# Attention values by one 129-column product for three of four blocks, and normalised outputs written by the vector engine

## The reference, cut to what matters

```python
x = x + s * g                      # first layer: linear attention, experts, routed experts
xn = _layernorm(x)
s = _L1_attn_ref(xn, qkv, q_bias, positional, out_kernel, out_bias)   # the stage changed
g = _silu(_L1_ffn_ref(xn, W_r, W_k, W_v, mu_r, mu_k))
x = x + s * g
```

## Time and profile before

| what | value |
|---|---|
| time, median of 3 runs | 1228.07 us (1223.23 to 1232.13) |
| profiled execution | 1229.18 us, of which the span is 1227.2 us |
| mean granted TensorE clock | 0.985 |
| TensorE products busy | 1162.7 us (95%) |
| VectorE busy | 821.1 us (67%) |
| GpSimd busy | 825.2 us (67%) |
| ScalarE busy | 681.0 us (55%) |

### The profile page before, as it was taken

The page is one execution under the profiler, slowest core; times in us unless marked ns, Lnnn a source line. Parts: engine busy times, 40 slices in busy tenths (PEclk is TensorE's granted clock), DMA queues, the critical chain, the costliest instruction groups (busy, mean ns, idle before and its releaser), DMA issues.

```text
span 1227.2 us, 31272 instructions
## 1 busy us (share of the span) xinstructions
PE 1162.7 (95%) x11854; PEld 762.0 (62%) x11862; DVE 821.1 (67%) x2026; ACT 681.0 (55%) x1374; POOL 825.2 (67%) x1097
## 2 busy tenths in 40 slices
PE   4899899989898999999999999999999999999997
PEld 2355466757574666766666666676666666566665
DVE  3778768613476786687578668668757866866552
ACT  2534343226414566666656666666665666666665
POOL 1778300130516588798797788888879879888895
PEclk9999889989999999999999999999999999999998
DMA  8200200022103402222031140221203104023001
GB/s 319 115 1 1 74 5 1 9 69 77 36 14 77 117 15 45 44 55 45 19 79 24 23 88 10 45 58 41 45 19 79 36 11 88 11 45 68 14 2 36
DMA packets 74753, 60.10 MB, mean 49 GB/s; under 512 B 38950, under 2 KB 69162, under 8 KB 73516
## 3 DMA queue, kind: packets, MB, share of 16 engines
q1 hardware_dynamic: 73580, 56.02, 18.5%
q0 software_dynamic: 1024, 2.09, 0.6%
HBM read 19.70 MB, written 4.72 MB: 20 GB/s over the span
## 4 chain that ended last, share of the span: by engine, by line
PE 66%; ACT 2%; DVE 2%; issue 1%; DVEq 0%
PE S L1875 10%; PE S L1876 10%; PE S L1877 9%; PE A L1865 9%; PE O L1889 5%; PE O L1890 5%; PE O L1887 5%; PE M L1856 2%; PE M L1833 2%; PE M L1835 2%; PE M L1834 2%; PE M L1850 1%; PE M L1843 1%; PE M L1841 1%; PE M L1842 1%
## 5 line engine op out<-in xcount | busy, mean ns | idle before, releaser
L1617 POOL TENSOR_TENSOR plow<-prob 128x512 f16<-128x512 f32 (+3 forms) x640 | 589.1, 932 | 93.6 <-ACT prob L2091 70.0
L2091 ACT ACTIVATE prob<-S,keep_sigma 128x512 f32<-128x512 f32 (+3 forms) x640 | 396.1, 626 | 264.5 <-PE S L1877 261.6
L2192 DVE CUSTOM_DVE_ANT_0 junk<-A,mask_rows,part 128x512 bf16<-128x512 f32 (+3 forms) x384 | 249.0, 648 | 98.1 <-PE A L1865 77.6
L1887 PE MATMUL O<-V,prob 128*128 128x65 f16 x2176 | 232.7, 193 | 0.2 <-POOL plow L1617 0.2
L1889 PE MATMUL O<-V,prob 128*128 128x64 f16 x2176 | 232.5, 194 | 0.0
L1890 PE MATMUL O<-V,plow 128*128 128x65 f16 x2176 | 231.6, 192 | 0.0
L1875 PE MATMUL S<-rows 97*128 97x512 f16 (+3 forms) x640 | 223.1, 349 | 3.8 <-ACT prob L2091 3.5
L1865 PE MATMUL A<-rows 96*128 96x512 f16 (+3 forms) x640 | 221.0, 346 | 1.3 <-DVE part L2192 1.0
L1876 PE MATMUL S<-rows 96*128 96x512 f16 (+3 forms) x640 | 222.3, 347 | 0.0
L1877 PE MATMUL S<-rows 96*128 96x512 f16 (+3 forms) x640 | 220.7, 345 | 0.0
L1887 PEld LDWEIGHTS O<-V,prob 128*128 128x128 bf16 x2176 | 203.0, 97 | 23.6 <-POOL plow L1617 0.3
(11 more groups left out here) (365 smaller groups left out, 1880.8 us busy)
## 6 DMA issues: line engine op xcount, KB each, us to landing
rows<-stage_rows SPq DMA_DIRECT2D x64, 256.0 KB, 3.4
V<-stage_v SPq DMA_DIRECT2D x16, 516.0 KB, 4.7
W<-in_W SPq DMA_DIRECT2D x2, 2048.0 KB
shifted<-turned SPq DMA_DIRECT2D x32, 128.0 KB, 2.3
rows<-stage_pos SPq DMA_DIRECT2D x64, 64.0 KB, 3.1
w<-in_w SPq DMA_DIRECT2D x2, 1024.0 KB
xe_rows<-zero SPq DMA_DIRECT2D x1, 1280.0 KB, 9.1
ye_rows<-xe SPq DMA_DIRECT2D x5, 256.0 KB, 3.2
```

The lines of the kernel that those rows point to most:

```text
L1617: pool.tensor_tensor(plow[:, k % PB, 0:w], full, full.bitcast(BF16).rearrange("p (q e) -> p q e", e=2)[:, :, 1], ALU.subtract).then_inc(s_ ...
L1887: pe.matmul(both, high[:, cs, 1], vh[h][:, j, 0:HS + 1], start=(j == 0 and s == 0), stop=False, skip_group_check=True)
L2091: act.activation(prob[:, k % PB, 0:w], S[k % 2][:, 0:w], ACT.Exp, scale=sigma[:, 2 * p + h:2 * p + h + 1]).then_inc(s_exp, 1)
L2192: dve.tensor_tensor_reduce(junk[:, g % 2, 0:w], A[g % 2][:, 0:w], add, -1.0, before, ALU.add, ALU.min, out).then_inc(s_max, 1)
```

## The change

The `O` bank now holds, for the blocks s = 0, 1, 2 (APART = 3), 129 columns each (64 sums of high values, the sum of weights, 64 sums of low values) and for block 3 the 65 columns as before; 3 x 129 + 65 = 452 of 512 columns. For the three blocks the two products with high weights become one of 129 columns. ScalarE no longer writes outputs: `scaled` is gone. VectorE, in the slot where it inverted the sums (m+8), takes two inversions, scales the low part and the high part of three blocks, scales block 3, and adds the low part.

```diff
+APART = TPC - 1
+        lows = sb("low_outputs", [P, APART, HS])
                 for s in range(r, TPC):
                     cs = slice((s - r) * P, (s - r + 1) * P)
-                    at = s * (HS + 1)
+                    at = s * VW
                     both, part = O[c % 2][:, at:at + HS + 1], O[c % 2][:, at:at + HS]
-                    pe.matmul(both, high[:, cs, 1], vh[h][:, j, 0:HS + 1], start=(j == 0 and s == 0), stop=False,
-                              skip_group_check=True)
-                    pe.matmul(part, high[:, cs, 1], vh[h][:, j, HS + 1:VW], start=False, stop=False, skip_group_check=True)
+                    if s < APART:
+                        pe.matmul(O[c % 2][:, at:at + VW], high[:, cs, 1], vh[h][:, j, :], start=(j == 0 and s == 0), stop=False,
+                                  skip_group_check=True)
+                    else:
+                        pe.matmul(both, high[:, cs, 1], vh[h][:, j, 0:HS + 1], start=False, stop=False, skip_group_check=True)
+                        pe.matmul(part, high[:, cs, 1], vh[h][:, j, HS + 1:VW], start=False, stop=False,
+                                  skip_group_check=True)
                     ins = pe.matmul(both, plow[:, n % PB, cs], vh[h][:, j, 0:HS + 1], start=False, stop=j == TPC * c + s,
                                     skip_group_check=True)
...
-            def scaled(p, m):
...
-                act.wait_ge(s_rec, g + 1)
-                for s in range(TPC):
-                    ins = act.activation(otok[:, TPC * c + s, HS * h:HS * (h + 1)],
-                                         O[c % 2][:, s * (HS + 1):s * (HS + 1) + HS], ACT.Copy,
-                                         scale=rsum[:, c % 2, s:s + 1])
-                ins.then_inc(s_otok, 1)
...
-                if n >= SCALE:
-                    scaled(*divmod(n - SCALE, SLOTS))
...
                     dve.wait_ge(s_pv, SLOTS * p + m + 1)
-                    sums = O[c % 2][:, 0:TPC * (HS + 1)].rearrange("p (s v) -> p s v", v=HS + 1)[:, :, HS]
-                    dve.reciprocal(rsum[:, c % 2, :], sums).then_inc(s_rec, 1)
+                    g = 2 * NC * p + NC * h + c
+                    blocks = O[c % 2][:, 0:APART * VW].rearrange("p (s v) -> p s v", v=VW)
+                    last = O[c % 2][:, APART * VW:APART * VW + HS]
+                    r, to = rsum[:, c % 2, :], otok[:, TPC * c:TPC * (c + 1), HS * h:HS * (h + 1)]
+                    each = r[:, 0:APART].unsqueeze(2).to_broadcast([P, APART, HS])
+                    dve.reciprocal(r[:, 0:APART], blocks[:, :, HS])
+                    dve.reciprocal(r[:, APART:TPC], O[c % 2][:, APART * VW + HS:APART * VW + HS + 1]).then_inc(s_rec, 1)
+                    dve.wait_ge(s_rec, g + 1)
+                    dve.wait_ge(s_otok, g + 1)
+                    if h == 0 and c == 0:
+                        dve.wait_ge(s_item, count(turn_item(plan[p == PAIRS - 1], -1, 3), p)[0])
+                    dve.tensor_tensor(lows[:], blocks[:, :, HS + 1:VW], each, ALU.mult)
+                    dve.tensor_tensor(to[:, 0:APART, :], blocks[:, :, 0:HS], each, ALU.mult)
+                    step(dve.tensor_scalar(to[:, APART, :], last, r[:, APART:TPC], None, ALU.mult))
+                    dve.tensor_tensor(to[:, 0:APART, :], to[:, 0:APART, :], lows[:], ALU.add).then_inc(s_otok, 1)
```

## The result

| kernel | median us | against the kernel before, 95% interval |
|---|---|---|
| before | 1229.33 (6 runs) | |
| changed | 1237.57 (6 runs, 1234.35 to 1239.25) | 1.0068 (1.0049 to 1.0087) |

A forecast was written before the change was run, and what follows sets the result against it. TensorE's back-to-back stream of products was taken as the bound. 1229.18 - 8.4 (merged product) + 2.4 (VectorE's group work) - 0 (ScalarE) - 0.8 (end) = 1222.4, given as 1222 us; range 1215 to 1237 us.

The forecast's parts named there:

- Part 1, the product: TensorE's value products: a merged block takes 87.0 ns, 5.5 less, over 1536 blocks; gain 8.4 us, range 0 to 10.3.
- Rivals 3 and 4: Merged product: 3, it saves nothing, 1231 us, chance 0.14; 4, its weight load is unhidden, 1270 us, chance 0.02.
- Part 2, the price of the group work: VectorE's added work at group ends: 1.32 us net per group, bounds 1.2 and 1.7, 64 groups, 84 us.
- the surcharge of the addition: VectorE's 192-column addition, both inputs in SBUF, beside a working GpSimd: 0.04 us on top of 0.28, at worst 0.16.
- Part 2, the path: TensorE waiting on VectorE's delayed maxima near slots 7 and 19: 0.3 to 0.35 us a pair, 2.4 us in all.
- The capacity of the `A` link: Row-score products wait for the maximum of two tiles before; slots 19 and 7 can take 1.2 us each.
- several slots: Items and joins behind the delayed maxima on VectorE's queue have this long until someone needs them.
- Part 3, ScalarE's stall: Slot 50 of each pair: the 0.6 us stall goes, but VectorE's maximum holds the same time; value 0, at most 4.9 us.
- The end: Last inversion to transpose: 2.28 us before, then 1.41 us and a signal of 0.06; 0.8 us less.
- Rival 1: VectorE becomes the bound at the eight group ends; with 2.0 us net per group 1248 us; chance 0.14.

The follow-up runs named there:

- e1: The changed kernel with only the merging undone (high weights of blocks 0 to 2 take two products again); 1243.73 us, ratio 1.0117.
- e2: The kernel before with the merged product alone; ScalarE writes outputs as before, low part left out for blocks 0 to 2; 1222.33 us, ratio 0.9955.
- e4: The changed kernel with the addition folded into three 64-column VectorE instructions that take the high part from PSUM, same result; 1226.36 us, ratio 0.9982.
- e3: The changed kernel without VectorE's last addition, so the low part is left out of the outputs; 1222.17 us, ratio 0.9952.
- e5: The changed kernel with VectorE only copying the low part and adding the high part from the bank, ScalarE scaling one slot later; 1222.82 us, ratio 0.9944.

## Why the prediction was wrong

**Part 1, the product: right, a fifth too much.** The merged block is 87 ns as forecast. Over a pair the value products give 0.83 us, which is 6.6 us for eight pairs, not 8.4. The difference is in the blocks left alone: between other blocks block 3 takes 95.4 ns from start to start where it took 92.0, and as the last of a stretch its first two distances are 66.3 ns against 61.7. In e1, with the same bank layout but no merged product, it is 92.0 again, so it comes with the merged products; why is open. e1 (6.2, with 6.8 in the value products) and e2 (5.4 against the run of before beside it, 6.5 in the stage) agree with 6 to 7. Rivals 3 and 4 fell: products of 129 columns with a load each stand 57.6 ns from the next. This also disagrees with the 81 ns that the Trainium skill, "TensorE: Matmul & The Clock Gate", section "Back-to-back issue gap", gives for 128 columns in such a stream.

**Part 2, the price of the group work: this is the step that failed.** The term was the surcharge of the addition, "scaled to 192 columns that is 0.04, at worst 0.16". The rows that I scaled had 64 x 512 elements and a median of 805 ns against 692, and I took the difference for a slower rate. It is a wait for GpSimd's instruction to end; it doesn't shrink with the columns. Measured: a mean of 0.23 us, 0.5 at slot 19 and 0.7 at slot 51.

The trace of the kernel before had it already. One of the 28 instructions of the earlier trace rows, and GpSimd beside it:

```profile
659.16 1.03 DVE L2166 TENSOR_TENSOR shifted<-turned,shifted 64x512 f32<-64x512 f32 x1
```

```profile
658.60 1.04 POOL L1617 TENSOR_TENSOR plow<-prob 128x512 f16<-128x512 f32 x1 [0.48 <-ACT prob L2091]
```

GpSimd ends at 659.64 and the join at 660.19. 27 of the 28 last, within 7 ns, the longer of 674 ns and what GpSimd's instruction still needs plus 542 ns. Only the part behind the wait shrinks with the columns, from 542 ns for 512 to 214 for 192; the median of 805 was a mixture of instructions that waited and that did not.

The rest of the sum held: 1.38 us without the surcharge, against 1.37 in mine. Inside it block 3 took 0.31 us for 0.24, since 208 ns was the price with a constant and not with a pointer scalar, and the inversions and scalings were 0.06 cheaper. The Trainium skill, "SBUF — State Buffer", section "Who interferes with whom", says that a VectorE instruction with two SBUF inputs contends with a GpSimd instruction that reads SBUF, and that the order of issue decides who blocks; that the first one holds the shared ports for its whole instruction it says of VectorE's 2-port modes. I cited it for the kind and not for the amount. The trace agrees, and shows the whole instruction for two SBUF inputs too: ends 0.21 to 0.24 us behind GpSimd's in 51 of 56 cases.

**Part 2, the path: right in the link, short by one.** The capacity of the `A` link holds nearly: at slot 19 I had 1.2 us; the net work there was 1.29 + 0.5 = 1.8 and the stall 0.68, which makes it 1.1, and e4 gives the same (1.33 net, 0.23 of stall). But the list had only the `A` buffers. The banks `M`, which VectorE frees with its item instructions, add 0.42 us a pair; I had given these "several slots". With both links slot 19 takes only about 0.8 us from the first inversion to the next maximum: work of 1.88 us (changed kernel), 1.42 (e4) and 0.98 (e3) delays TensorE there by 1.06, 0.61 and 0.16 us. That e5, planned against 1.2 us, stays clear with its 0.78 is in part luck.

**Part 3, ScalarE's stall: right.** It went, and came back as a wait on the maximum at the next slot; in e3 it is all that is left. **The end: right.** Inversion to transpose went from 2.28 us to 1.62, for the forecast 1.5:

```profile
1225.96 0.18 DVE L2261 RECIPROCAL rsum<-O 128x3 f32<-128x3 f32 x1 [3.35 <-PE O L1896]
```

```profile
1227.58 0.63 PE L1852 MATMUL M<-keep_ident,otok 128*128 128x128 f32 x4 [1.66 <-DVE otok L2270]
```

**Which case came true.** Rival 1, with its mechanism, its place and even its half microsecond, but at the tight places alone, so that it stopped at 0.7% and not above 1%. Summed over the eight pairs, from the first score product of each, the stage is 8.5 us longer; the end is 0.8 shorter, and 1.3 us more stand ahead of the stage, where nothing was changed. That is the 9.0 us between the spans. The part ahead of the stage differs between the eight profiled executions from 414.9 to 420.0 us with the same code, so its 1.3 us say nothing of the change.

**A second effect of the same kind.** VectorE's own position joins, the instructions of the earlier trace rows, also have two inputs in SBUF. The added work moves them against GpSimd: their mean rises from 815 to 1043 ns in the changed kernel, 0.9 us a pair. In e3 and e5 it is 930 and 928 ns, so half of that rise comes without a loss of time; what the other half costs is not shown.

## What to carry to other kernels

- Before a VectorE instruction with two inputs in SBUF is put beside a busy GpSimd, charge it with the rest of GpSimd's current instruction, not with a percentage. The earlier trace rows had shown this in min, median and max; the two timelines side by side tell the cause. Take one input from PSUM if the data lie there anyway.
- An engine that is busy 82% of the time can stop one that never rests by a burst. List for each place of the burst what the links behind it can take, and all links: here tile buffers, item banks and the transposes, each with another distance.
- Where a change has a paying and a paid part, try the split first: e5 keeps the merged product and moves the rest off the tight engine.

## What the runs showed of the hardware

- A VectorE instruction with two SBUF inputs that starts while GpSimd is in an instruction ends 0.21 to 0.24 us after that instruction's end (51 of 56 cases, 192 columns; the other five were hardly touched). For 512 columns it is 0.54 us in the kernel before. One that starts free takes 357 ns, as does the same with one input in PSUM, whatever GpSimd does (357 to 359 in 64 cases, e5). The other way the price is small: a `plow` of 512 columns that starts while an addition has 0.25 us to go takes about 1.15 us instead of 1.04 (16 cases).
- A small VectorE instruction from PSUM, 64 columns, takes 275 ns with a pointer scalar (changed kernel; 276 in e4) and 208 with a constant. The first multiplies and the second adds; no run changes the scalar alone.
- A block of three small products took 95.4 ns between merged blocks and 92.0 between blocks of its own kind, in the same bank layout (e1); no run here says why.
